# One group of sixteen for the two key halves of a head group, with the small groups and projection halves placed anew

## The reference, cut to what matters

```python
xl = layer_norm(x, ln_l_g, ln_l_b);  xg = layer_norm(x, ln_g_g, ln_g_b)
local[:, 0:32] = mha(xl[:, 0:32], ...)    # over 32 rows of each sequence
glb            = mha(xg, ...)             # 32 sequences, 256 queries, 256 keys
x = layernorm(x + local + glb)
# mha: 16 heads of 8 numbers; softmax over the keys; product with the values; output projection
x = layernorm(x + moe(x))                 # top-1 of 8 experts, 1024 places each
```

## Time and profile before

| | |
|---|---|
| median of 3 runs | 719.67 us (717.74 to 720.22) |
| the profiled execution, its own time | 713.15 us |
| its span from first to last instruction | 711.4 us |
| granted TensorE clock, mean | 0.949 |
| busy: TensorE, VectorE, ScalarE, GpSimd | 89%, 79%, 68%, 63% of the span |
| chain that ended last | TensorE 58%, VectorE 27%, issue 6%, DMA 4%, ScalarE 2% |

### The profile page before, as it was taken

The page is one execution under the profiler, slowest core; times in us unless marked ns, Lnnn a source line. Parts: engine busy times, 40 slices in busy tenths (PEclk is TensorE's granted clock), DMA queues, the critical chain, the costliest instruction groups (busy, mean ns, idle before and its releaser), DMA issues.

```text
span 711.4 us, 18732 instructions
## 1 busy us (share of the span) xinstructions
PE 633.0 (89%) x6430; PEld 353.5 (50%) x6430; DVE 561.1 (79%) x1722; ACT 485.8 (68%) x1095; POOL 445.1 (63%) x813
## 2 busy tenths in 40 slices
PE   3478999999999999999999999999999369999993
PEld 2344554445454454444544444444444237677682
DVE  7566899999999999999899998998972206776776
ACT  2226678888888988888878888888888234354431
POOL 5414434578788787787877877675667702544546
PEclk9657999999999999999999999999999569999997
DMA  5696889975648747666466565673401022333321
GB/s 114 157 214 173 215 232 194 249 178 124 168 134 184 176 99 208 165 140 164 111 158 179 120 160 144 131 176 73 86 26 35 27 65 73 108 97 105 96 86 40
DMA packets 143960, 95.70 MB, mean 135 GB/s; under 512 B 11885, under 2 KB 139718, under 8 KB 143865
## 3 DMA queue, kind: packets, MB, share of 16 engines
q1 hardware_dynamic: 138728, 85.82, 50.2%
q0 software_dynamic: 4096, 7.81, 3.8%
q10 hardware_dynamic: 1040, 0.87, 0.5%
HBM read 47.70 MB, written 45.74 MB: 131 GB/s over the span
## 4 chain that ended last, share of the span: by engine, by line
PE 58%; DVE 27%; issue 6%; DMA 4%; SPq 2%; POOL 2%; ACT 2%; DVEq 0%; POOLq 0%; ACTq 0%
DVE mx L1040 15%; PE ps_o L613 11%; PE ps_b L586 9%; PE ps_a L1487 7%; PE ps_b L1481 4%; PE ps_a L568 4%; PE ps_m L644 3%; PE ps_f L522 3%; PE ps_m L659 2%; PE ps_f L517 2%; PE ps_f L527 2%; PE ps_a L1481 2%; PE ps_f L1481 2%; PE ps_m L638 2%; DVE rest L1012 2%
## 5 line engine op out<-in xcount | busy, mean ns | idle before, releaser
L1040 DVE TENSOR_REDUCE mx<-ps_a 128x2 f32<-128x512 f32 (+1 forms) x576 | 360.3, 654 | 44.9 <-PE ps_a L568 43.1
L839 ACT ACTIVATE prob<-ps_b 128x512 f32<-128x512 f32 (+1 forms) x576 | 301.2, 580 | 66.4 <-PE ps_b L586 65.3
L568 PE MATMUL ps_a<-ks,qs 56*128 56x256 bf16 (+1 forms) x1152 | 186.0, 272 | 12.0 <-DMA ks<-stack 6.2
L586 PE MATMUL ps_b<-qs,ks 59*128 59x256 bf16 (+1 forms) x1152 | 187.7, 269 | 6.5 <-DMA qs<-mT 1.7
L613 PE MATMUL ps_o<-prob,vp 128*32 128x256 f32 (+1 forms) x2304 | 170.2, 379 | 0.4 <-ACT prob L839 0.4
L586 PEld LDWEIGHTS ps_b<-qs,ks 59*128 59x128 bf16 x1152 | 80.5, 95 | 105.2 <-ACT prob L839 64.5
L1631 POOL DMA_INDIRECT out<-res,dest x64 | 62.3, 973 | 76.5 <-DVE res L1604 61.1
L1334 POOL DMA_INDIRECT routed<-row,slot x64 | 67.2, 1050 | 47.7 <-issue 27.4
L568 PEld LDWEIGHTS ps_a<-ks,qs 56*128 56x128 bf16 x1152 | 75.2, 95 | 25.2 <-DVE mx L1040 13.1
L613 PEld LDWEIGHTS ps_o<-prob,vp 128*32 128x32 f32 x2304 | 49.1, 108 | 57.1 <-issue 48.6
L1487 PE MATMUL ps_a<-w_sb,prob 128*128 128x128 f32 x512 | 59.7, 275 | 2.1 <-ACT prob L1539 2.1
(11 more groups left out here) (153 smaller groups left out, 999.2 us busy)
## 6 DMA issues: line engine op xcount, KB each, us to landing
stack<-part SPq DMA_DIRECT2D x36, 384.0 KB, 3.3
qs<-stack SPq DMA_DIRECT2D x72, 192.0 KB
ks<-stack SPq DMA_DIRECT2D x72, 192.0 KB
stack<-part SPq DMA_DIRECT2D x36, 256.0 KB, 3.6
stack<-part SPq DMA_DIRECT2D x36, 128.0 KB, 4.3
routed<-empty SPq DMA_DIRECT2D x8, 520.0 KB, 4.6
rows_sb<-routed SPq DMA_DIRECT2D x16, 260.0 KB, 3.9
xt<-x SPq DMA_DIRECT2D x16, 256.0 KB, 3.1
```

The costliest lines, as they stand in the source:

```text
L568: ins = nc.tensor.matmul(ps_a[:, n % 3, qt * S:qt * S + keys.stop - keys.start], qs[half, b, hp, qt * P:(qt + 1) * P], ks[half, b, hp, key ...
L586: ins = nc.tensor.matmul(ps_b[:, 1 - e, kt * n:(kt + 1) * n], ks[half, u % STACKS, hp, kt * P:(kt + 1) * P], qs[half, u % STACKS, hp, quer ...
L839: nc.scalar.activation(prob[:, hp, half * n:(half + 1) * n], ps_b[:, half, 0:n], ACT.Exp).then_inc(exp_done, 1)
L1040: nc.vector.reduce_max(mx[:, u % 2, :, col], ps_a[:, n % 3].rearrange("p (t k) -> p t k", t=2)[:, :, 0:k], axis=AX).then_inc(max_done, 1)
```

## The change

For TensorE, a slot now holds both key halves of a head group one behind the other wherever the next step allows it:

| slot | value products before | after | other work that moves |
|---|---|---|---|
| 0 | (u-1, 3, 0) | even steps with a pair: none; else as before | `turn_x` comes here from slot 1 |
| 1 | (u-1, 3, 1) | even steps with a pair: (u-1, 3, 0), (u-1, 3, 1); else as before | |
| 2 | | | first query half comes here, ahead of `turn_o`; the second half of the value projection leaves |
| 3 | (u, 0, 0) | (u, 0, 0), (u, 0, 1) | first query half leaves |
| 4 | (u, 0, 1) | none | second half of the value projection comes here |
| 5 | (u, 1, 0) | none | |
| 6 | (u, 1, 1), (u, 2, 0) | (u, 1, 0), (u, 1, 1) | first key half comes here |
| 7 | (u, 2, 1) | (u, 2, 0), (u, 2, 1) | first key half leaves |

ScalarE: `scale_shift` moves up, ahead of `copy_counts` and `copy_o`. `second_part`, one copy of the remainders of queries and keys, becomes two: `second_part_q` in the even step after exponential 6, `second_part_k` in the odd step after exponential 2. `place_v(second, 0)` moves from behind exponential 3 to behind 4, `place_v(second, 1)` from behind 4 to behind 5, and `norm_again` in the odd steps with a pair from behind 5 to behind 6. VectorE: `take_rest_k` moves from (2, 0) to (1, 1), ahead of `gate`. The amount of work stays the same but for the one copy that becomes two; no DMA is added or moved.

```diff
             if hp == 0:
-                if there(u - 1):
+                if first is not None:
+                    turn_x(first, 0)
+                    turn_x(first, 1)
+                elif there(u - 1):
                     p_v(u - 1, 3, 0)
             if hp == 1:
                 if there(u - 1):
+                    if first is not None:
+                        p_v(u - 1, 3, 0)
                     p_v(u - 1, 3, 1)
...
-                if first is not None:
-                    turn_x(first, 0)
-                    turn_x(first, 1)
             if hp == 2:
                 if second is not None:
                     project_in(second, "v", 0)
-                    project_in(second, "v", 1)
+                if first is not None:
+                    project_in(first, "q", 0)
...
             if hp == 3:
                 if there(u):
                     p_v(u, 0, 0)
+                    p_v(u, 0, 1)
...
-                if first is not None:
-                    project_in(first, "q", 0)
             if hp == 4:
-                if there(u):
-                    p_v(u, 0, 1)
...
+                if second is not None:
+                    project_in(second, "v", 1)
                 if first is not None:
                     project_in(first, "q", 1)
             if hp == 5:
-                if there(u):
-                    p_v(u, 1, 0)
...
-            if hp == 6 and there(u):
-                p_v(u, 1, 1)
-                p_v(u, 2, 0)
+            if hp == 6:
+                if there(u):
+                    p_v(u, 1, 0)
+                    p_v(u, 1, 1)
+                if first is not None:
+                    project_in(first, "k", 0)
             if hp == 7:
                 if there(u):
+                    p_v(u, 2, 0)
                     p_v(u, 2, 1)
                 if first is not None:
-                    project_in(first, "k", 0)
                     project_in(first, "k", 1)
```

```diff
+        def second_part_q(p):
+            act.wait_ge(rest_q, upto(p))
+            nc.scalar.copy(part_of(p, 1), by_unit(rest[:, 0]))
+
+        def second_part_k(p):
+            act.wait_ge(rest_k, upto(p))
+            nc.scalar.copy(part_of(p, 4), by_unit(rest[:, 1])).then_inc(part1_ready, 1)
...
                 exponential(u, 1)
+            if first is not None:
+                scale_shift(first)
             if routes(u - 3):
                 copy_counts(u - 3)
             if there(u - 1):
                 copy_o(u - 1)
             if there(u):
                 exponential(u, 2)
-            if first is not None:
-                scale_shift(first)
             if second is not None:
-                second_part(second)
+                second_part_k(second)
...
             if there(u):
                 exponential(u, 6)
+            if first is not None:
+                second_part_q(first)
...
-            if at == (1, 1) and routes(u - 3):
-                gate(u - 3)
-            if at == (2, 0):
+            if at == (1, 1):
                 if second is not None:
                     take_rest_k(second)
+                if routes(u - 3):
+                    gate(u - 3)
```

More of the change, by code:

```diff
@@ L913, in step @@
                 copy_max(u + 1)
-            if second is not None:
-                place_v(second, 0)
             if routes(u - 2) and batch(u - 2) >= 3:
@@ L928, in step @@
             if second is not None:
-                place_v(second, 1)
+                place_v(second, 0)
             if there(u):
                 exponential(u, 5)
-            if routes(u - 2):
+            if second is not None:
+                place_v(second, 1)
+            elif routes(u - 2):
                 norm_again(u - 2)
@@ L935, in step @@
                 exponential(u, 6)
+            if first is not None:
+                second_part_q(first)
+            if second is not None and routes(u - 2):
+                norm_again(u - 2)
+            if there(u):
                 exponential(u, 7)
@@ L1136, in fill @@
                 gate_sum(u - 3)
-            if at == (1, 1) and routes(u - 3):
-                gate(u - 3)
-            if at == (2, 0):
+            if at == (1, 1):
                 if second is not None:
                     take_rest_k(second)
+                if routes(u - 3):
+                    gate(u - 3)
+            if at == (2, 0):
                 if late is not None:
```

## The result

The changed kernel took **709.34 us** (median, 706.53 to 711.29) against 719.94 us for the kernel before in the same series of runs (717.74 to 722.88): ratio 0.9856, 95% interval 0.9822 to 0.989. It is faster, by 10.6 us. The forecast was 25 us. So the sign held, and less than half of the size arrived; the time lies inside the range, near its upper end.

The account below looks back on a forecast made before the run. TensorE and VectorE alternately set the pace, with VectorE's floor at 26.2 us a pair. Saving 0.9 + 1.3 - 0.1 - 0.3 = 1.8 us a pair gives 20.7, plus 2.0 + 2.0 + 0.6 = 25.3: 719.67 to 694.4 us, range 686 to 713.

Parts of the forecast that it names:

- A: Even step's `turn_max` to the odd step's first reduction, chain on TensorE: 9.38 us to become 8.5, 0.9 saved a pair.
- B: Odd step's first reduction to its first of slot 6: 10.78 us to become 9.5, 1.3 saved a pair.
- C: Odd step's slot 6 reduction to the next even step's `norm_o` end: 8.58 us, all VectorE, plus 0.1 for `turn_o`.
- Five visits fewer: TensorE's groups of value products joined, five fewer a pair: 0.7 us less, net 0.5 after 0.18 for float32 operations.
- Light steps: Steps 31 to 34, without projections: 0.5 us saved a step, 2.0 in all, bounds 0 and 4.6.
- The early pairs: The 3.5 pairs before step 7, with fewer VectorE tasks: 0.6 us saved each, 2.0 in all, bounds 0 and 6.3.
- The last steps: Steps without maxima, where two groups are joined and moved: 0.6 us saved; the expert tail untouched.
- rival 1: Only half the gain arrives, about 1 us a pair, 706 us; a sign is `take_rest_k` waiting for `first_part_k`; chance 0.20.
- rival 4: Slower: `copy_turned` ends late in slot 5, so `logits` holds the next scores; +16 us, 735 us; chance 0.10.
- Rival 2: Only grouping counts, an unseen ring of waits keeps the pace: 0.5 us a pair, 713 us; chance 0.08.
- moves at nothing: ScalarE operations and `scale_shift` move almost free: 0.3 us a pair lost to score products waiting for their second bank.
- sign of being wrong: If VectorE's idle time only moves, the same 2.1 us a pair, the balance of the slots was not the cause.

Follow-up runs that it names:

- plain_after: Changed kernel with each indirect scatter DMA replaced by a plain DMA to consecutive places, rows not placed by expert: 692.22 us, median pair 27.01 us.
- split_o1: Changed kernel with the second indirect DMA of each scatter one step later and two `o1` buffers: 693.65 us, 0.9707 of the kernel before.
- plain_before: Kernel before the change with its indirect scatter DMAs replaced by plain ones, rows not placed by expert: 710.18 us, median pair 28.78 us.
- late_before: Kernel before the change with both scatter DMAs issued one step later; the text gives no total time, step 7 begins at 147.8 us.
- after_o1: Changed kernel with two buffers for the default output rows `o1`, scatter left in place: ratio 0.985 to the kernel before, 28.03 us a pair.
- one_indirect: Changed kernel with the second indirect DMA of each scatter made a plain one to rows nobody reads: 27.02 us a pair.
- after_gap: Changed kernel with two GpSimd operations of 1.05 us between the two indirect DMAs of a scatter: 29.65 us a pair.
- late_o1: Changed kernel with both scatter DMAs one step later and two `o1` buffers: ratio 0.9733 to the kernel before, 27.35 us a pair.
- late_after: Changed kernel with both scatter DMAs one step later, behind the routing places, and one `o1` buffer; the text gives no total time.

## Why the prediction was right and where it failed

- **The bound was read rightly.** In `plain_after` the pair is 27.01 us with VectorE idle 0.52 and 0.23 us; with 0.09 for each spell, its own work is 27.01 - 0.75 - 0.18 = 26.1 us, the forecast floor 26.2.
- **A and B: right to 0.1 us each**, 8.50 and 9.55 against 8.5 and 9.5, in the changed kernel too. The balance of the slots was the cause of both. C without the hold is 8.97, against 8.58 + 0.1 and the 0.3 for ScalarE, which could fall anywhere.
- **Five visits fewer: right**, 14 to 9. Their worth was mis-sized, 0.5 us against 0.8 measured, and the placing 1.3 against 1.0; the sum of both, 1.8 against 28.78 - 27.01 = 1.77, hides that, which is luck. The 0.18 us that I set against the grouping, for float32 operations ahead of the scores, isn't needed to explain the 0.8. The Trainium skill's rule, page "TensorEngine Tiling (Array Packing)", section "Key Properties", had given an estimate of 0.3 to 0.4 us for three fewer changes of mode; neither it nor my count reaches what was measured, and no run here tells the two ways of counting apart.
- **Light steps: right without the hold.** The timeline of `plain_after` has the distance that ScalarE allows, 487.72 - 485.32 = 2.40 us from `turn_max` to `logits`, forecast 2.4; the four steps lost 2.2 us, forecast 2.0. With the hold all of it is gone, 52.1 us.

```profile
485.32 0.29 PE L623 MATMUL ps_m<-ident_bf,mpart 128*48 128x128 bf16 x2
...
487.72 0.61 PE L659 MATMUL ps_m<-wg_sb,turned_T 128*128 128x8 f32 x4
```

- **The early pairs: wrong.** Step 7 begins at 147.6 us instead of 145.3, where 2.0 us less were forecast. TensorE's timeline shows one new wait of the size of the whole forecast gain and more, where the kernel before has none over 0.85 us:

```profile
78.89 0.28 PE L586 MATMUL ps_b<-qs,ks 59*128 59x128 bf16 x1 [3.58 <-DMA qs<-mT]
```

  The chain behind it is SP's queue, issuing DMA after DMA from 70.06 to 75.17, and then the transfer of the maxima, 3.63 us. `plain_after` has it too (3.37 us), `split_o1` has three of 1.30, 0.77 and 1.11 us instead. I had named the DMA waits of this part and then put 0.6 us a pair on it as if there were none. How much the change has to do with them stays open: step 7 begins at 144.8 and 147.8 us in `plain_before` and `late_before`, too, and at 144.3 to 149.0 in the kernels with the new order.
- **The last steps and the tail** gave nothing that can be seen: from step 34 to the end 186.0 us instead of 183.8, forecast 0.6 less. That stretch differs by several us between kernels whose tails are alike (181.6 in `plain_after`, 185.4 in `split_o1`), so no reading hangs on it. The whole of it doesn't tell where the medians' 10.6 us are: the profiled execution of the kernel before lay 6.8 us under its median of 719.94, that of the changed kernel 2.0 us over its own, and between the two profiled ones there are 1.9 us.
- **Rivals.** `take_rest_k` never waited for `first_part_k` (rival 1), and `logits` did not hold TensorE for `copy_turned` (rival 4). Rival 2 gave the measured size, 0.57 us a pair for its 0.5, and even its words, a pace kept by something "that I haven't seen"; but its reason, that only the grouping counts, is false where no hold is: there the placing is worth 1.0 us. That the sizes agree is luck.
- **One bound was added up wrongly.** The upper bounds together, 28.8 + 4.6 + 6.3 + 0.6 = 40.3 us, lead to 679 us and not to 684. The measured time lies at the other end, and nothing hangs on it.

**The step that failed** is the sum for a pair, 1.8 us, and in it the part "moves at nothing". It asked of each moved operation which engine would wait for it, put 0.3 us a pair on banks, and took it for granted that a matmul's consumers start when the matmul ends. What it left out is the delay between the two. In the odd steps of the changed kernel the slot whose scores VectorE and ScalarE both need at once stands beside GpSimd's two indirect DMAs, and there the increments come up to 1.7 us late. Its price, against the kernel with plain DMAs: 28.16 - 27.11 = 1.05 us a pair over steps 7 to 30 as means, 12 us in all, and 2.4 us in the light steps; on one and the same chip, 28.14 - 27.02 = 1.1 us in the median pair (`after_o1` and `one_indirect`). The rows of the kernel before could not have shown it: their trace has no late increment. The median of 719.94 us, from which the forecast was counted down, may have some in it, and then it is part of both kernels.

The account of the profiled executions, where 25.3 us had been forecast and 1.9 were measured: 20.7 - 6.5 = 14.2 us are missing in steps 7 to 30, 2.0 + 0.1 = 2.1 in the light ones, 2.0 + 2.3 = 4.3 before step 7 and 0.6 + 2.2 = 2.8 behind step 34, 23.4 in all. The hold is 12.1 + 2.4 = 14.5 of them. By the medians 14.7 us are missing; how they are made up no trace shows. That the two figures are so near proves nothing. Without a hold the forecast is not reached either: from `plain_before` to `plain_after` it is 710.18 - 692.22 = 18.0 us by the times, not 25.3, and 19.9 us between the two profiled spans, 18.5 of them in steps 7 to 30.

The prediction had named a sign of being wrong: idle time of VectorE that only moves. The page of the changed kernel shows just that, 47.0 us of waiting for `ps_a` where it was 43.1. Taken by itself it would have condemned the balance of the slots, which the kernels without a hold bear out. It was the exchange of one DMA for another that told the two apart.

**What is shown and what is not.** Shown, on one chip: with two close indirect DMAs of GpSimd the increments come late and the median pair takes 28.14 us (`after_o1`); with one of the two or with plain ones and a busy GpSimd it takes 27.02 and 27.01. Shown in the changed kernel's own trace: VectorE and ScalarE stand idle until the late increments arrive. Shown by the two kernels with plain DMAs: without a hold, grouping and placing are worth the forecast 1.8 us a pair. Argued only: that the matmuls of the hold had really been executed on time; their starts are recorded, their ends are modelled, but the increments of 1.55 us of recorded work, from +1.19 to +2.74, came within 0.33 us. Not shown: that the new order of TensorE's work is a condition, that the kernel before has no hold in its timed runs, and that splitting the pair (`split_o1`, `after_gap`) takes a hold away. Open: why some executions show it and others with the same work beside the same DMAs don't, and what in the chip is held. To settle the first, both kernels would have to be profiled on one chip that shows the hold and on one that doesn't.

## What to carry to other kernels

Where a consumer starts later than its matmul's end in the timeline, look at the semaphore increments and at what the other engines issue in that window, before calling it a slow matmul; the chain of waits books it on the producer. When a reordering gives less than a sum that was right elsewhere, exchange the one suspected operation for a cheap one of the same place in both kernels: the difference of the differences tells a wrong sum from a loss on top. Do it on the chip where the effect was seen, with the original kernels beside it, and check on a stretch that is the same in all kernels, here the tail, that the traces are of one kind. And two indirect DMAs of GpSimd that can stand apart are worth trying apart: here taking one of them away was worth 1.1 us of 28.1 in each pair of steps, and the kernel with the two apart, which needed a second buffer where their place was tied to a store, ran in 0.9707 of the time of the kernel before.

## What the runs showed of the hardware

- In some executions TensorE's semaphore increments come late beside two indirect DMAs of GpSimd, the first at time 0, the second at 1.43 us. In the changed kernel an increment due at 0.95 us was on time and those due from 1.19 us on came at 2.77 us or later in 23 of 26 steps, up to 1.67 us late; ScalarE's and VectorE's went on. The same was seen in all five kernels with such a pair on chips 0 and 7, and in none of the three on chips 12 and 6, beside the same work of TensorE (`late_o1` and `late_after`).
- On chip 7 one indirect DMA with a plain one directly behind it made increments at most 0.28 us late, and two plain ones, each behind a GpSimd operation of 1.05 us, none.
- An indirect DMA of 128 rows occupies GpSimd for 0.97 to 1.15 us, a plain one of the same bytes for 0.61 us on average.
- A visit to a group of eight value products costs 0.16 us beyond its matmuls in this kernel (0.8 us for five), against 0.14 us by the earlier trace rows.
